# Two constant bf16 matmuls ahead of each edge column's matmuls in the two convolutions of a graph network

## What is computed

```python
def _rgcn_conv(x, src, dst, etype, basis, comp, root, bias):
    W = jnp.einsum('rb,bio->rio', comp, basis)             # one 128x128 matrix for each of 8 relations
    seg = dst * r + etype
    agg = jax.ops.segment_sum(x[src], seg, num_segments=n * r)
    cnt = jax.ops.segment_sum(jnp.ones_like(seg, x.dtype), seg, num_segments=n * r)
    mean = (agg / jnp.maximum(cnt, 1.0)[:, None]).reshape(n, r, -1)
    return jnp.einsum('nri,rio->no', mean, W) + x @ root + bias

h = _rgcn_conv(x, src, dst, edge_type, basis1, comp1, root1, bias1)
h = jax.nn.relu(h)
out = _rgcn_conv(h, src, dst, edge_type, basis2, comp2, root2, bias2)
```

## Time and profile before

| | |
|---|---|
| median of 3 runs | 8123.53 us |
| the profiled execution, its own time | 8061.14 us |
| its span, first to last instruction | 8059.4 us |
| TensorE busy | 5700.8 us (71%) |
| GpSimd busy | 5215.1 us (65%) |
| VectorE busy | 4131.7 us (51%) |
| ScalarE busy | 2089.4 us (26%) |
| mean granted TensorE clock | 0.738 of full speed |

### The profile page before, as it was taken

One profiled execution on the slowest core, in us unless ns is written; L12 is line 12 of the kernel. 1 busy time (PEld: TensorE's weight loads), 2 busy tenths in 40 slices (PEclk: granted clock), 3 DMA queues, 4 the chain that ended last, 5 costly groups with the idle time before them and its releaser, 6 DMA issues. The chain is left out here.

```text
span 8059.4 us, 106968 instructions
## 1 busy us (share of the span) xinstructions
PE 5700.8 (71%) x28365; PEld 4156.6 (52%) x28365; DVE 4131.7 (51%) x13390; ACT 2089.4 (26%) x4143; POOL 5215.1 (65%) x5105
## 2 busy tenths in 40 slices
PE   5776777778888876777777777666566676666656
PEld 3443444447777766555555555554454555444444
DVE  6555555558888864444444444444333333333333
ACT  5555555554444433111111111111000000000000
POOL 3555555568888875666666666664666666666665
PEclk9888888889999987566666666667556656666666
DMA  5445555459999975111111111111111111111121
GB/s 150 138 138 135 137 140 143 126 129 188 191 191 191 190 150 169 50 51 51 51 50 51 51 51 51 51 51 41 50 52 51 52 51 51 52 51 51 51 52 44
DMA packets 816560, 748.84 MB, mean 93 GB/s; under 512 B 126421, under 2 KB 719249, under 8 KB 815637
## 3 DMA queue, kind: packets, MB, share of 16 engines
q1 hardware_dynamic: 578020, 401.11, 19.0%
q0 software_dynamic: 237296, 340.25, 18.5%
q10 hardware_dynamic: 630, 0.39, 0.0%
HBM read 574.58 MB, written 165.86 MB: 92 GB/s over the span
## 5 line engine op out<-in xcount | busy, mean ns | idle before, releaser
L2168 POOL DMA_INDIRECT got<-h_dram,etcol x3322 | 3140.1, 945 | 1736.2 <-issue 959.2
L2290 DVE SCALAR_TENSOR_TENSOR hacc<-bank,hacc 128x256 f32 (+1 forms) x3322 | 1180.8, 355 | 2770.0 <-remote 1416.5
L2180 PE MATMUL bank<-share,got 128*128 128x128 f32 x4436 | 1171.6, 403 | 696.5 <-DVE hacc L2290 439.2
L2180 PEld LDWEIGHTS bank<-share,got 128*128 128x128 f32 x4436 | 959.6, 281 | 1143.6 <-issue 1066.9
L1653 POOL DMA_INDIRECT msg_dram<-total,idx x1008 | 969.9, 962 | 733.7 <-ACT total L1270 438.1
L1668 POOL DMA_INDIRECT acc_dram<-total,idx x653 | 1023.0, 1567 | 211.6 <-issue 202.5
L2207 PE MATMUL bank<-rcnt,chosen 7*128 7x512 f32 (+45 forms) x784 | 720.2, 1016 | 411.2 <-issue 296.1
L2180 PE MATMUL bank<-hot,got 128*128 128x128 f32 x2208 | 585.2, 403 | 317.9 <-DVE hacc L2290 229.0
L2199 PE MATMUL bank<-wrel,umade 128*128 128x128 f32 x3136 | 674.3, 402 | 157.4 <-issue 93.2
L2233 ACT ACTIVATE hacc<-ones_f 128x2048 f32<-128x2048 f32 (+1 forms) x196 | 290.8, 1483 | 1892.1 <-DVE umade L2305 1006.2
L2180 PEld LDWEIGHTS bank<-hot,got 128*128 128x128 f32 x2208 | 478.4, 281 | 544.3 <-issue 517.6
(11 more groups left out here) (273 smaller groups left out, 8855.4 us busy)
## 6 DMA issues: line engine op xcount, KB each, us to landing
edges<-in_edge_attr SPq DMA_DIRECT2D x415, 256.0 KB
unit<-msg_dram SPq DMA_DIRECT2D x616, 129.0 KB
got<-h_dram,etcol POOLq DMA_INDIRECT x3322
low<-rows_dram SPq DMA_DIRECT2D x164, 256.0 KB
win<-split_dram SPq DMA_DIRECT2D x416, 96.0 KB
low<-rows_dram SPq DMA_DIRECT2D x252, 128.0 KB
acc_dram<-zeros SPq DMA_DIRECT2D x200, 128.0 KB
made<-acc_dram SPq DMA_DIRECT2D x147, 128.0 KB, 3.1
```

Source lines behind the costliest of these rows:

```text
L2168: pool.indirect_dma_start(got[k][:, j, :], None, g.h_dram[which][:, :], bass.IndirectOffsetOnAxis(ap=source[:, c:c + 1], axis=0)).then_inc ...
L2180: ins = nc.tensor.matmul(columns[j][:, 0:P], got[k][:, j, :], equal, start=True, stop=True)
L2290: v.scalar_tensor_tensor(to, columns[j].rearrange("p (a n) -> p a n", n=NARROW), 1.0, to, ALU.mult, ALU.add).then_inc(s_sum, 1)
```

## The change

In front of each column's matmuls TensorE multiplies `ones3` by the first 256 columns of `bias3`, twice, into numbers 256 to 511 of the column's bank. To be allowed to, it first waits for VectorE to be done with the bank (`s_sum`), so that this wait now stands ahead of the waits for the gathers (`s_got`, once for each group) and for the matrix (`s_node`). The two matmuls raise no semaphore.

```diff
         def own_tensor(pe):
+            def keep_warm(j):
+
+                for _ in range(2):
+                    nc.tensor.matmul(g.bank[j][:, 2 * P:], g.ones3[:, :], g.bias3[:, 0:2 * P], start=True, stop=True)
+
             def sum_columns(group):
                 k, n = group % NGA, g.columns(group)
-                pe.wait_ge(s_got[k], group // NGA * (16 * TG) + 16 * n + got_before[k])
                 for j in range(n):
                     c = group * TG + j
+                    need(pe, s_sum, c - (TG - 1))
+                    keep_warm(j)
+                    if j == 0:
+                        pe.wait_ge(s_got[k], group // NGA * (16 * TG) + 16 * n + got_before[k])
                     pe.wait_ge(s_node, c + 1)
-                    need(pe, s_sum, c - (TG - 1))
                     equal = hot[group % NHOT][:, j, :]
                     ins = nc.tensor.matmul(columns[j][:, 0:P], got[k][:, j, :], equal, start=True, stop=True)
```

## The result

The changed kernel takes 8166.73 us (median of 8 runs, 8161.28 to 8200.15), the kernel before beside it on the same chip 8124.59 us (8 runs, 8121.22 to 8155.24): a ratio of 1.0051, 95% interval 1.0037 to 1.0064. It is 42 us slower, where 117 were forecast. Sign and order of size are right, the forecast's own range (8140 to 8588 us) holds the time, and neither rival came. The profiled execution of after takes 8162.45 us, 4 us under its median, that of before 8061 us, 62 us under its own and 60 us under the shortest of its 8 runs: the two traces lie 101 us apart, and some 60 us of these don't come from the change.

What follows compares the result with a forecast made beforehand. The loop TensorE, VectorE, TensorE was taken to bound the kernel, with late signals. Terms 0 + 117 + 0 + 0 on 8061 gave 8178 us, or 8240 us against the median; range 7650 to 8700 us, likeliest case 8140 to 8588 us.

Steps and rivals of the forecast that it cites:

- What bounds the kernel: Both convolutions: the loop TensorE, VectorE, TensorE bounds them, two thirds work and one third late signals.
- GpSimd's floor: Both convolutions: 3322 gathers at 1.245 us each need at least 4136 us.
- the 748 us: Both convolutions: the gap between the gathers' 4136 us and the 4884 us taken, about GpSimd's 777 us of waits.
- The added matmuls: Ahead of each column's matmuls: a pair takes 0.43 us at half clock, 1428 us in all.
- TensorE's work now: TensorE in the convolutions: the clock rises from 0.63 to 0.80, busy time from 3316 to 3668 us, 352 us more.
- rival A: Convolutions: the clock stays up and late signals go, so the kernel is faster, 7690 us; chance 0.31.
- rival C: Convolutions: the clock stays at 0.63, 1243 us of work added, 659 us arrive, 8782 us; chance 0.15.
- How much of it counts: Convolutions: a third of TensorE's 352 us of added busy time reaches the end, 117 us.
- The moved wait: TensorE's wait at `s_sum`, now ahead of `s_got`: cost 0, since all three waits must pass in both kernels.
- VectorE and PSUM: The column's bank: the pair writes it while VectorE reads other banks, cost 0.
- Rival B: Convolutions: late signals and GpSimd's pauses set the pace, so no difference, within 16 us of 8123 us; chance 0.11.
- What was said to show it: Changed profile's convolutions: TensorE near 3670 us, clock near 0.80, GpSimd's waits about 890 us, VectorE's idle time mostly "remote".

Runs made afterwards that it cites:

- e1: The changed kernel without the added matmuls, only the moved wait; signals on time: ratio 1.0003 to the kernel before.
- g1: The changed kernel with one added matmul per column in place of two; signals late: 8136.70 us, ratio 1.0017 to the kernel before.
- f1: The changed kernel itself, run again with signals on time: 6959.29 us against 6969.14 us, ratio 0.9986 to the kernel before.
- g2: The changed kernel with the pair behind all three waits; signals late: 8191.53 us, ratio 1.0082 to the kernel before.
- e2: The changed kernel with both added matmuls cut to one partition in place of 128; signals on time: ratio 1.2311 to the kernel before.
- e3: The changed kernel with four added matmuls per column in place of two; signals on time: ratio 0.9990 to the kernel before.
- h2: The changed kernel with half the gathers, its output not the convolution's; signals late: 6424.43 us, ratio 0.7908 to the kernel before.

## Why the prediction was right in sign and too high in size

**What bounds the kernel.** GpSimd's floor is confirmed: with signals on time the gathers of both convolutions span 4193 us (e1) for a forecast floor of 4136 us. The rest of the 748 us goes with the late signals, for e1 is 0 against the kernel before on time and its gathers wait 32 us for TensorE in place of 777. What the prediction couldn't see is that the late signals come and go with the chip and the gathers, and not with TensorE's clock (0.63 with them, 0.64 without).

**The added matmuls.** Right: 0.42 us for a pair at half clock for 0.43, 0.22 at the full clock.

**TensorE's work now: the first step that failed.** 352 us more were forecast, and 210 us came (3527 us for 3668 us). The clock is not the reason: 0.77 for 0.80, a middle that was chosen and came near. The conversion is. The prediction takes the full clock's share of the *time* (0.26, 0.60) as if it were a share of the *work*, and so writes 3316 / (1 - 0.26/2) and 5240 x 0.70. Work goes with busy time times clock: 3316 us at 0.63 are 3316 x 0.63 / 0.5 = 4178 us at half clock, with the added 1428 us 5606 us, and at 0.80 these take 5606 x 0.5 / 0.80 = 3504 us, 188 us more than before. A third of them is 63 us and not 117. (By the same slip rival A's 539 us less should have been 426, and rival C's 1243 us more 1133.) With signals on time this sum comes out to the microsecond, in part by luck: 3202 x 0.64 / 0.5 + 1428 = 5527 us, x 0.5 / 0.85 = 3251 us, measured 3251; with four matmuls, 3585 us for 3509. With late signals and the measured 0.77 it gives 3640 us, 113 us too many. The mean clock of a stretch isn't the clock that the matmuls had, as it weighs idle time like work: split by the clock record of the traces, TensorE is busy for 614 us at the full level and 2702 us at the half level before, and for 1729 and 1798 us after, mean clocks of 0.59 and 0.75 for its busy time, and the work rises by 1324 us at half clock for the 1428 forecast.

**How much of it counts: the second.** A third of the added busy time was to arrive. By the medians it was 42 of 210 us, a fifth. The 210 us are the traces', though, and the trace of before is one of an execution that was 62 us short; trace against trace, 101 us arrive. Surer is the step from g1 to the changed kernel, whose traces both lie within 5 us of their medians: 173 us more busy time (3354 to 3527 us) and 30 us more time, a sixth. The third, taken from a comparison of two convolutions that differ in more than TensorE's work, was too much. The two steps together are the miss: 352 x 1/3 = 117 us, 210 x 1/5 = 42 us. The reading that fits all runs, argued from them rather than shown by one: TensorE's work costs nothing while GpSimd sets the pace (f1, 0.9986), and something where late signals have used up its slack (1.0017 for one matmul, 1.0051 for two). That the sign came out right hangs on the chip: in f1, the one set with signals on time in which the change was run, it is the other way.

**The moved wait.** 0 was forecast. By itself it is 0 in four sets, all with signals on time (0.9997 to 1.0003). With late signals it wasn't run by itself; g1 leaves little room for a price (13 us with one matmul), and g2 shows that the pair ahead of the other waits is some 25 us cheaper than behind them, of which the prediction said nothing.

**VectorE and PSUM.** 0 was forecast; the adds take 355 ns in the changed kernel as in the kernel before, and 354 ns in e1 for 356 in f1, so the pair beside them takes nothing from them.

**Rival A** needed a clock over 0.87 and the late signals gone. The clock was 0.77, and 1353 of 1416 us of late signals were left. Its second half came true in a way that has nothing to do with the change: on other chips the signals come in time, also in e1, which has no added matmul. The rule that the prediction weighed, from the Trainium skill (TensorE: Matmul & The Clock Gate, Part 1), that activity releases the clock, agrees with the doses here: 0.64, 0.85 and 0.97. e2 doesn't bear it out as it stands: TensorE is busy there for 5722 of 5750 us at a clock of 0.54. What it doesn't do in this kernel is bring time, as e3 shows (clock 0.97, time 0.9990).

**Rival B**, within 16 us, is what g1 gives for half the dose (13 us). Two matmuls are past it.

**Rival C** was the clock that doesn't rise. With full tiles it rises. e2 is this rival made real, with tiles of one row: not the 8.1% that 659 us would be, but 23%, on a chip with signals on time, since TensorE, busy for all but 28 us, becomes the bound.

**What was said to show it.** TensorE near 3670 us: 3527. Clock near 0.80: 0.77. GpSimd's waits near 890 us: 888, which is luck, as 60 of the 101 us between the traces don't come from the change. VectorE's idle time mostly "remote": 1353 of 2843 us, its largest part and less than half.

**Open:** what makes TensorE's signals late in some sets; how the late signals turn TensorE's added work into time, since no run takes them away from the full kernel on a late chip; whether a pause of GpSimd would let them through; the moved wait alone and four matmuls with late signals. No variant beats the kernel before on a chip with late signals; on time f1 and e3 beat it by 0.1%.

## What to carry to other kernels

Ask first which engine's pace sets the time. Matmuls that only keep TensorE busy raised its clock here. They gained where TensorE's own work was the limit (h2, 107 us, part of it perhaps from fewer late signals), next to nothing where another engine set the pace (f1, 0.9986), and cost a little in the kernel with late signals (1.0051). If such matmuls are tried, give them all 128 partitions, put them ahead of the waits, and measure on more than one chip, since a ratio from a chip with late signals doesn't hold on one without. When a busy time is carried from one clock to another, multiply it by the clock and divide by the new one, and take the clock of the busy time where the trace gives it.

## What the runs showed of the hardware that was not expected

- The same kernel takes 8123 us in some sets, each on one chip, and 6965 us in others. In the convolutions the difference is TensorE's signals, whose effect on VectorE and GpSimd comes up to 6 us after the matmuls; in the other sets no such wait is left. Single instructions take the same in both (a gather 945 and 947 ns, an add 355 and 354 ns). The layer before is shorter too: the first gather starts at 2750 us in place of 3150 us. With half the gathers nearly all of the late signals in the convolutions go (1416 us to 126 us).
- Matmuls of one partition don't raise the granted clock (0.54, for 0.64 without any and 0.85 with 128 partitions), and a column's two full matmuls behind them take 0.59 us in place of 0.43 us, their weight load no longer beside the stream before it.
